# Masked attention with residual and LayerNorm on one core: the last two pairs' probabilities transposed by TensorE, and the ending's products in another order

## The reference

```python
q = _heads(x @ Wq + bq); k = _heads(x @ Wk + bk); v = _heads(x @ Wv + bv)
scores = jnp.einsum('bhqd,bhkd->bhqk', q, k) / np.sqrt(64)
probs = jax.nn.softmax(scores + jnp.where(adj, 0.0, -9e15)[:, None], axis=-1)
ctx = jnp.einsum('bhqk,bhkd->bhqd', probs, v)       # heads put side by side again
out = _layernorm(x + ctx @ Wf + bf, axis=-1)        # no scale, no shift
```

## Time and profile before

| | |
|---|---|
| median of 3 runs | 1035.22 us (1034.44 to 1036.75) |
| profiled execution, its own time | 1036.09 us |
| its span, first to last instruction | 1034.2 us |
| mean granted TensorE clock | 0.997 of full |
| busy in the span | PE 98%, DVE 71%, POOL 61%, ACT 57% |
| stretch 989 to 1034.2 | the ending |

### The profile page before, as it was taken

How to read it: one execution, slowest core, us unless ns; L and a number is a source line. 1 busy time by engine, 2 the same in 40 slices (tenths; PEclk the granted TensorE clock), 3 DMA queues, 4 the chain that set the end, 5 groups by cost and what they waited for, 6 DMA issues and landing times.

```text
span 1034.2 us, 26752 instructions
## 1 busy us (share of the span) xinstructions
PE 1018.6 (98%) x7161; PEld 906.7 (88%) x7161; DVE 734.0 (71%) x2826; ACT 592.9 (57%) x2119; POOL 626.8 (61%) x649
## 2 busy tenths in 40 slices
PE   8999999999999999999999999999999999999995
PEld 7889889888889888888898898898898898888885
DVE  3677776777677677777777777767776777776775
ACT  4565655655656646646556556556556466466551
POOL 1355666666656665665656656666566566656674
PEclk9999999999999999999999999999999999999998
DMA  7386676676676676666666766766766766765444
GB/s 196 79 210 178 173 197 163 176 189 163 177 190 163 180 189 166 186 181 167 189 174 172 194 167 173 196 162 175 191 161 174 195 164 182 185 167 171 152 141 139
DMA packets 340570, 179.63 MB, mean 174 GB/s; under 512 B 222656, under 2 KB 324160, under 8 KB 340544
## 3 DMA queue, kind: packets, MB, share of 16 engines
q1 hardware_dynamic: 339744, 178.94, 63.4%
q10 hardware_dynamic: 800, 0.39, 0.1%
HBM read 103.75 MB, written 75.50 MB: 173 GB/s over the span
## 4 chain that ended last, share of the span: by engine, by line
PE 96%; DVE 1%; DMA 1%; ACT 0%; issue 0%; POOL 0%; SPq 0%; POOLq 0%; DVEq 0%; ACTq 0%
PE qk_ps L377 14%; PE qk_ps L379 13%; PE qk_ps L378 13%; PE cov_ps L377 13%; PE cov_ps L379 13%; PE cov_ps L378 13%; PE scores_ps L393 9%; PE cov_ps L408 9%; DMA p_out<-p_turned 1%; DVE s_mask L572 1%; PE qk_ps L468 0%; POOL probs L870 0%; SPq L289 0%; DVE xT_lo L561 0%; ACT probs L755 0%
## 5 line engine op out<-in xcount | busy, mean ns | idle before, releaser
L755 ACT ACTIVATE probs<-s_mask,neg_max 128x128 f32<-128x128 f32 x768 | 297.5, 391 | 6.2 <-DVE neg_max L578 5.5
L870 POOL TENSOR_TENSOR probs<-probs,inv_sum 128x768 f32<-128x768 f32 x128 | 188.9, 1476 | 81.5 <-DVE inv_sum L591 81.5
L572 DVE CUSTOM_DVE_ANT_0 s_mask<-scores_ps,mask_bias 128x128 f32<-128x128 f32 x768 | 172.5, 286 | 91.5 <-PE scores_ps L393 86.5
L865 POOL TENSOR_SCALAR y_sb<-y_sb,mean_var,rstd 128x384 f32<-128x384 f32 x124 | 204.9, 1652 | 22.9 <-POOL rstd L859 22.9
L584 DVE STREAM_TRANSPOSE p_turned<-probs 128x768 f32<-128x768 f32 x128 | 125.2, 978 | 114.2 <-POOL probs L870 114.0
L859 POOL TENSOR_TENSOR rstd<-var_eps,minus_half 128x1 f32<-128x1 f32 x128 | 72.0, 563 | 181.8 <-DVE var_eps L619 181.8
L772 ACT ACTIVATE qT<-qk_ps,bq_col 128x512 f32<-128x512 f32 x96 | 65.5, 682 | 155.5 <-PE qk_ps L379 155.5
L755 ACT ACTIVATION_READ_ACCUMULATOR probs<-s_mask,neg_max 128x1 f32 x768 | 145.0, 189 | 0.0
L748 ACT CAST cT_hi<-cov_ps 128x384 fp32r<-128x384 f32 x128 | 61.5, 480 | 137.2 <-PE cov_ps L408 134.3
L561 DVE TENSOR_TENSOR xT_lo<-xT,xT_hi 128x384 fp32r<-128x384 f32 x120 | 113.1, 980 | 32.8 <-ACT xT_hi L742 32.7
L377 PE MATMUL cov_ps<-wf_hi,cT_hi 128*128 128x384 f32 x384 | 129.9, 338 | 1.7 <-DVE cT_lo L546 1.7
(11 more groups left out here) (64 smaller groups left out, 1988.5 us busy)
## 6 DMA issues: line engine op xcount, KB each, us to landing
p_out<-p_turned SPq DMA_DIRECT2D x128, 384.0 KB, 2.6
pT<-p_out SPq DMA_DIRECT2D x512, 96.0 KB, 2.4
x_in<-in_x SPq DMA_DIRECT2D x128, 192.0 KB, 3.6
out<-y_sb SPq DMA_DIRECT2D x128, 192.0 KB, 2.5
x_blocks<-in_x SPq DMA_DIRECT2D x360, 64.0 KB, 2.3
adj_u<-in_adj SPq DMA_DIRECT2D x32, 64.0 KB, 3.4
probs<-in_L_gnn_Wv SPq DMA_DIRECT2D x1, 576.0 KB, 6.2
pT<-in_L_gnn_Wf SPq DMA_DIRECT2D x1, 576.0 KB, 6.7
```

Of the source, the lines that this page charges most:

```text
L572: last = nc.vector.tensor_tensor_reduce(out=s_mask[:, e, h, :], in0=scores_ps[:, score_cols(e, h)], in1=mask_bias[:, e, :], scale=SCALE, s ...
L755: last = nc.scalar.activation(probs[:, e, h, :], s_mask[:, e, h, :], ACT.Exp, bias=neg_max[:, e, h:h + 1], scale=1.0, accum_out=row_sum[:, ...
L865: nc.gpsimd.tensor_scalar(y_sb[:, y, :], y_sb[:, y, :], mean_var[:, e, 0:1], rstd[:, e, 0:1], ALU.subtract, ALU.mult).then_inc(y_ready, 1)
L870: nc.gpsimd.tensor_tensor(probs[:, e, :, :], probs[:, e, :, :], inv_sum[:, e, :].unsqueeze(2).broadcast_to([P, HEADS, SEQ]), ALU.mult).the ...
```

## The change

For sequences 124 to 127 the turn by DVE, the store to device memory and the four loads are gone. TensorE transposes the six 128x128 matrices (**T n**, `transpose_p`) into the member's own two score banks, once M of sequence 126 or 127 has read them, and ACT copies the two banks into `pT` (`copy_pT`, two copies a sequence). Pair b's probabilities get a tile of their own, `last_probs`, in the place of `p_turned`, so that E126 need not wait for pair a. C126 and C127 go into `qk_ps` instead of `cov_ps`. The order of the ending is rewritten on all engines. On PE it is now: S124 S125, C120 C121, S126 S127, O120 O121, V124 V125, C122 C123, T124 T125, O122 O123, C124 C125, V126 V127, T126 T127, O124, C126 C127, O125, O126, O127. On SP the ten stores of y follow each other with nothing between. On POOL the order is P124, P125, y 120, P126, y 121, P127, the residual inputs of 126 and 127, y 122, y 123. The body of the loop is as it was.

```diff
+        def ctx_bank(e, n):
+            return qk_ps[e] if isinstance(n, int) and n >= 2 * (ENDING + 1) else cov_ps[e]
+        def pT_bank(e, half):
+            return scores_ps[:, (2 * e + half) * BANK:(2 * e + half) * BANK + MATS * SEQ]
...
             def ending():
                 a, b = ENDING, ENDING + 1
                 load_blocks(a // TURN, a % TURN - 1, 1, 2 * (a - 1) + 1)
-                for e in range(2):
-                    store_y(a - 3, e)
-                for q in (a, b):
-                    i, c = q // TURN, q % TURN
-                    store_blocks(c, 0, 2 * q)
-                    load_blocks(i, c, 0, 2 * q)
-                    store_blocks(c, 1, 2 * q + 1)
-                    if q == b:
-                        for e in range(2):
-                            store_y(a - 2, e)
-                    load_blocks(i, c, 1, 2 * q + 1)
-                for q in (a - 1, a, b):
+                for q in (a - 3, a - 2, a - 1, a, b):
                     for e in range(2):
                         store_y(q, e)
...
             def ctx_product(i, c, p, e):
                 n, at = 2 * (p - LAG) + e, 2 * (c - LAG) + e
-                past(pe, pT_landed[at % PT_RING], 2 * i + at // PT_RING, per=BLOCKS * DMA)
+                if isinstance(n, int) and n >= BY_VECTOR:
+                    pe.wait_ge(pT_copied, 2 * (n - BY_VECTOR + 1))
+                else:
+                    past(pe, pT_landed[at % PT_RING], 2 * i + at // PT_RING, per=BLOCKS * DMA)
                 if isinstance(p, int) and p - 1 + AHEAD >= ENDING:
-                    past(pe, y_added, n - 2)
+                    past(pe, y_added, n - 2 if n < 2 * (ENDING + 1) else n - 4)
                     past(pe, v_copied, n)
...
+            def transpose_p(q, e, p_sb):
+                n = 2 * q + e
+                pe.wait_ge(probs_ready, n + 1)
+                pe.wait_ge(max_found, 2 * (ENDING + 1) + e + 1)
+                if q > ENDING:
+                    pe.wait_ge(pT_copied, 2 * (e + 1))
+                for h in range(HEADS):
+                    last = nc.tensor.transpose(pT_bank(e, h // MATS)[:, h % MATS * SEQ:(h % MATS + 1) * SEQ],
+                                               p_sb[:, e, h, :], ident[:, :])
+                last.then_inc(pT_done, 1)
...
+            def copy_pT(q, e):
+                n = 2 * q + e
+                act.wait_ge(pT_done, n - BY_VECTOR + 1)
+                past(act, ctx_done, n - PT_RING)
+                for half in range(2):
+                    nc.scalar.copy(pT[:, n % PT_RING, :, half * MATS:(half + 1) * MATS, :].rearrange(
+                        "p a h j -> p h a j"), pT_bank(e, half).rearrange("p (h a j) -> p h a j", h=MATS, a=BLOCKS)
+                        ).then_inc(pT_copied, 1)
```

More of the change, by code:

```diff
@@ L211, in attention_block @@
         xT_done = sem("xT_done")
+        pT_done = sem("pT_done")
+        pT_copied = sem("pT_copied")
         cT_split = sem("cT_split")
@@ L428, in out_product @@
                 pe.wait_ge(cT_split, n + 1)
+                if isinstance(n, int) and n >= 2 * (ENDING + 1):
+                    past(pe, y_added, n - 2)
                 split_product(cov_ps[e][:, 0:HID], lambda k: (
@@ L508, in ending, with at @@
             def ending():
                 a, b = ENDING, ENDING + 1
[L512 to L521, removed]
+                def at(q):
+                    return q // TURN, q % TURN, q
@@ new lines, in ending @@
+                for e in range(2):
+                    scores(a // TURN, a % TURN, e, 2 * a + e)
+                for e in range(2):
+                    ctx_product(*at(a), e)
+                for e in range(2):
+                    scores(b // TURN, b % TURN, e, 2 * b + e)
+                for e in range(2):
+                    out_product(a % TURN, a, e)
+                for e in range(2):
+                    late_v(a, e)
+                for e in range(2):
+                    ctx_product(*at(b), e)
@@ L522, in ending @@
+                for e in range(2):
+                    transpose_p(a, e, probs)
+                for e in range(2):
+                    out_product(b % TURN, b, e)
+                for e in range(2):
+                    ctx_product(*at(a + LAG), e)
                 for e in range(2):
                     late_v(b, e)
[L524 to L528, removed]
+                for e in range(2):
+                    transpose_p(b, e, last_probs)
@@ L530, in _ @@
+                out_product((a + LAG) % TURN, a + LAG, 0)
+                for e in range(2):
+                    ctx_product(*at(b + LAG), e)
+                out_product((a + LAG) % TURN, a + LAG, 1)
+                for e in range(2):
+                    out_product((b + LAG) % TURN, b + LAG, e)
             pe.wait_ge(ident_ready, 2)
@@ L692, in ending @@
-                invert_sums(1, 2 * a + 1)
+                for e in range(2):
+                    find_stats(a % TURN, e, 2 * (a - 2) + e)
+                invert_sums(0, 2 * b)
                 for e in range(2):
                     split_ctx(e, 2 * (a - 1) + e)
[L695 to L699, removed]
@@ L700, in ending @@
-                turn_blocks(*at(b), 0, 2 * b)
-                invert_sums(1, 2 * b + 1)
[L702 to L715, removed]
+                invert_sums(1, 2 * b + 1)
@@ new lines, in ending @@
+                for e in range(2):
+                    add_residual(*at(b), e, 2 * (a - 1) + e)
+                for e in range(2):
+                    find_stats(b % TURN, e, 2 * (a - 1) + e)
+                for e in range(2):
+                    split_ctx(e, 2 * a + e)
+                add_residual(*at(a + LAG), 0, 2 * a)
+                find_stats((a + LAG) % TURN, 0, 2 * a)
+                split_ctx(0, 2 * b)
+                add_residual(*at(a + LAG), 1, 2 * a + 1)
+                split_ctx(1, 2 * b + 1)
@@ L716, in ending @@
+                find_stats((a + LAG) % TURN, 1, 2 * a + 1)
+                for e in range(2):
+                    normalise_last(a, e)
+                for e in range(2):
+                    add_residual(*at(b + LAG), e, 2 * b + e)
+                    find_stats((b + LAG) % TURN, e, 2 * b + e)
                 for e in range(2):
@@ L811, in ending @@
                     exps(e, 2 * a + e)
+                exps(0, 2 * b, last_probs)
+                for e in range(2):
+                    copy_v(qk_ps[e], (2 * a + e) % V_RING, 2 * a + e)
                 for e in range(2):
```

51 lines of the change are left out of this document (29 added, 22 removed).

## The result

| | before | changed |
|---|---|---|
| median of 5 runs | 1035.22 us (1034.44 to 1036.75) | 1031.16 us (1030.56 to 1031.25) |
| ratio, 95% interval | | 0.9959 (0.9949 to 0.9970) |
| span of the profiled execution | 1034.2 us | 1029.3 us |
| mean granted clock | 0.997 | 0.999 |

A forecast was written before the change was run, and what follows sets the result against it. TensorE, busy 96%, was taken to bound the kernel. Its last product starting 6.0 us earlier, less 1.8 given back in the tail, made 4.2 us off the median: 1031.0 us, range 1029.2 to 1033.5 (8 in 10).

The forecast's parts named there:

- T: TensorE's transposes in the ending: 0.11 us each, 0.66 a sequence, 2.64 us added in all.
- The rule from the Trainium skill: Rival: transposes take about 275 ns each and don't engage full clock; time 1034.9 us, no change; chance 0.06.
- the prediction's 6.6 us: Cost of the ending's 24 transposes by the skill's rule, instead of 2.6, leaving nearly nothing of the gain.
- The new wait: TensorE ahead of C124, behind ScalarE's copies, E127, inversion I127 and residual R122: 1.03 us added.
- The tail: After O127 starts: late O125 puts N125 ahead of R126 on VectorE, R127 comes later; 1.8 us given back.
- the sum: TensorE up to its last output product: waits and half clock removed, less added costs; O127 starts 6.0 us earlier.
- C125 1.8: Old ending, TensorE ahead of C125: waiting for pT to land costs 1.8 us.
- C126 2.5: Old ending, TensorE ahead of C126: waiting for R124, itself behind a store of y, costs 2.5 us.
- C127 1.5: Old ending, TensorE at C127: waiting for loads of pT costs 1.5 us.
- half clock from there 2.2: Old ending, C127 and O126 on TensorE at 1.2 of 2.4 GHz: costs 2.2 us.
- The sum of 8.0: Old ending between the starts of O120 and O127: waits and half clock together cost 8.0 us of 32.4.
- -1.3 for S of pair 63: S126 and S127 moved into the gap before O120: 1.54 us off the later path, O120 starting 0.26 later.

The follow-up runs named there:

- e3: The changed kernel with each of the 24 transposes issued twice into the same place; 1034.17 us, ratio 0.9984 to the kernel before.
- e5: The kernel before with 20 unread transposes of the identity put between O125 and C126 on TensorE; 1034.22 us, ratio 0.9988 to the kernel before.
- e1: The changed kernel with residuals R122 and R123 ahead of inversion I127 on VectorE; 1030.20 us, ratio 0.9947 to the kernel before.
- e2: The changed kernel with O125 ahead of C126 and C127 on TensorE, R125 and St125 one place earlier on VectorE; 1030.38 us, ratio 0.9949 to before.
- e4: The kernel before with the stores of y 120 and y 121 moved ahead of loads in SP's queue; 1035.18 us, ratio 0.9997 to before.

## Why the prediction was right

**The amount.** 4.2 us was forecast, 4.45 is what the profiles have for the ending, 4.1 the medians.

**T.** Taken at 0.11 each, measured 0.107, and 0.109 by e3. The rule from the Trainium skill, "TensorE: Matmul & The Clock Gate", Part 4, has two halves. Its about 275 ns agrees as the duration of one transpose, whose median in the changed kernel is 273 ns; as a price in a row, which is how the prediction's 6.6 us used it, it doesn't hold, since the successor starts 0.11 after. That full clock doesn't engage disagrees with e5, where transposes took the place of idle time and the granted clock stayed at 1.00. In e3, with 24 in a row, it was 1.00 too. The prediction had read the clock's rise from the distances at the start of the kernel. The granted clock doesn't show that rise:

```profile
2.00:4.00 2.00, 1.96 (x10) 1.56 (x9) 0.00 (x0) 1.06 (x1) 0.00 (x0) 1.00 0.92 294
```

It is 1.00 already where the distance is 0.25. Why the first transposes are at half pace stays open, and the evidence on the clock is e5's.

**The new wait.** 1.03 was forecast ahead of C124, 0.98 came, by the links named: copies at 0.37 (0.385 taken), E127, I127, R122. That the 0.385 fitted is partly luck: it was the distance of two exponentials of 128x128, another operation on a third of the elements, and nothing in the rows tied a copy to it. A copy at the 0.467 of the rows would have put C124 0.33 later than forecast. C124 was put 18.57 behind S124's start (1008.48 - 989.91) and came 18.55 behind it. e1 showed that ScalarE's lateness reaches TensorE only through VectorE's order.

**The tail.** R127 was to stand 3.6 behind O127's start and stands 3.57 behind; e2 showed that O125's late place causes it: with O125 first it stands 2.00 behind (1020.85 to 1022.85).

**O127** came 6.27 earlier relative to S124 (1020.37 - 989.46 = 30.91 against 1027.09 - 989.91 = 37.18), where the sum had 6.0. The difference arose behind C124: from T126's start to O124's it took 1.22 (1012.71 to 1013.93), where the sum had 1.5, with small gaps that aren't there.

**What was wrong, without harm to the sum.** The list of what the old ending lost, "C125 1.8; C126 2.5; C127 1.5 ... half clock from there 2.2", was summed as if each item could be had by itself. The runs show otherwise. e4 took the 2.5 away and gained nothing, because the round trip of pT 127 holds the end whatever C126 does; e5 took half clock away and gained 1.5. The 1.5 put to C127 is also not all a wait: 0.70 is idle time, and the rest is C126 itself, already at half pace (1.55 for its twelve matmuls, where C125 has 0.88). The sum of 8.0 came out because the change removes the round trip, the stall and the fall of the clock together. That the time between two starts was split into shares by the gap that precedes each product, and not by what would be late next, is the error.

**What was not asked.** The forecast costed the new order only for what it adds to the chain. That the order as a whole costs 0.6 us, and that the same change without it would have been faster, was in its own numbers (-1.3 for S of pair 63, +1.0 for the wait, +1.8 given back in the tail, of which e2 recovered 1.0, as O126 then waits 0.52 for split 126) and wasn't drawn from them.

## What to carry to other kernels

Where an ending waits for round trips through device memory and TensorE has idle time, as here, transposing on TensorE at 0.11 us a 128x128 block can be worth more than its price: it took the landing out of the chain, and the clock stayed up. Of several waits on the way to one landing, taking away an early one gained nothing (e4); ask of each what would be late next. After a move to another engine, look again at what stands behind each wait in the strict order of the engines that were relieved: two small moves in the order gave 1.9 us more, against 4.5 for the change itself.

## What the runs showed of the hardware

The clock after idle time. In the kernel before, TensorE had no work for 2.47 us, and C126 behind that ran at half pace, granted 0.50 from 1020.3 on. In e4 C126 ran at full pace behind 0.21 us of idle time, and C127, behind 3.63, at half. Gaps of 1.74 and 1.79 in the kernel before, 0.98 in the changed kernel and 1.33 in e5 left the granted clock at 1.00. Twenty transposes of the identity, read by nothing, kept it at 1.00 in e5.

A wait for VectorE's semaphore can appear as "issue" in the trace: the 2.47 of the kernel before and the 0.98 of the changed one were waits for `y_added`, as e4 and e1 showed by taking away what set it late.

A transpose of a 128x128 float32 block lasts 0.27 us and takes 0.107 to 0.109 us of a row of them. ScalarE's copy of 128x384 out of PSUM into runs of 32 elements takes 0.37 us in a row of four.
